# Releasing an expert's weight transfers chunk by chunk in a mixture-of-experts stage

## What is computed

```python
xf = x.reshape(-1, x.shape[-1])
gate_logits = xf @ gate_w.T + gate_b
selected = jnp.argmax(softmax(gate_logits), axis=-1)
out = zeros
for j in range(8):
    yj = xf @ expert_w[j].T + expert_b[j]
    out = out + where((selected == j)[:, None], yj, 0.0)
```

## Time and profile before

| what | value |
|---|---|
| median of 3 runs | 1428.24 us (1428.13 to 1430.22) |
| the profiled execution's own time | 1424.34 us |
| its span, first to last instruction | 1422.7 us |
| mean granted TensorE clock | 0.993 |
| TensorE busy | 1385.2 us, 97% of the span |
| VectorE busy | 1136.3 us, 80% |
| ScalarE busy | 754.9 us, 53% |
| GpSimd busy | 213.2 us, 15% |
| DMA moved | 331.51 MB, 233 GB/s on average |

### The profile page before, as it was taken

The page is one execution under the profiler, slowest core; times in us unless marked ns, Lnnn a source line. Parts: engine busy times, 40 slices in busy tenths (PEclk is TensorE's granted clock), DMA queues, the critical chain, the costliest instruction groups (busy, mean ns, idle before and its releaser), DMA issues.

```text
span 1422.7 us, 20751 instructions
## 1 busy us (share of the span) xinstructions
PE 1385.2 (97%) x6881; PEld 1141.3 (80%) x6881; DVE 1136.3 (80%) x1119; ACT 754.9 (53%) x839; POOL 213.2 (15%) x234
## 2 busy tenths in 40 slices
PE   7899999999999999999999999999999999999996
PEld 7887888888888888888888888888766788788884
DVE  5868887878878788787887878877655799899994
ACT  5656555454554545545455454553204377677772
POOL 0111000000000000000000000000014266564462
PEclk9999999999999999999999999999999999999998
DMA  6864567477774777747676476765858746979951
GB/s 204 328 236 154 203 233 266 169 286 227 255 261 174 285 222 257 258 176 285 220 260 256 177 285 219 261 254 170 293 190 296 277 119 168 336 229 304 344 154 30
DMA packets 102938, 331.51 MB, mean 233 GB/s; under 512 B 15476, under 2 KB 23164, under 8 KB 102876
## 3 DMA queue, kind: packets, MB, share of 16 engines
q1 hardware_dynamic: 79556, 258.56, 49.0%
q0 software_dynamic: 23072, 71.85, 18.0%
q10 hardware_dynamic: 256, 0.40, 0.1%
HBM read 295.63 MB, written 46.14 MB: 240 GB/s over the span
## 4 chain that ended last, share of the span: by engine, by line
PE 91%; DVE 3%; DMA 2%; issue 1%; ACT 1%; ACTq 0%; SPq 0%; DVEq 0%; POOL 0%; POOLq 0%
PE pair L1140 27%; PE pair L1141 26%; PE pair L1142 26%; PE pair L1194 4%; PE pair L1416 1%; PE pair L1342 1%; PE pair L1333 1%; DVE wf L810 1%; DMA wraw<-exp_w 1%; PE pair L1221 1%; PE pair L1278 1%; PE pair L1204 1%; PE pair L1351 1%; PE pair L1383 1%; DVE wlr L1115 1%
## 5 line engine op out<-in xcount | busy, mean ns | idle before, releaser
L810 DVE TENSOR_TENSOR wf<-wf,term 128x1024 f32<-128x1024 f32 x308 | 376.7, 1223 | 65.8 <-ACT term L599 50.7
L599 ACT ACTIVATE term<-codes 128x1024 f32<-128x1024 int32 x308 | 320.6, 1054 | 139.4 <-DVE wf L810 139.4
L1140 PE MATMUL pair<-wh,hh 128*128 128x512 f32 x672 | 263.4, 392 | 3.2 <-DVE ring L873 1.4
L1141 PE MATMUL pair<-wl,hh 128*128 128x512 f32 x672 | 262.0, 390 | 0.0
L1142 PE MATMUL pair<-wh,hl 128*128 128x512 f32 x672 | 262.0, 390 | 0.0
L1140 PE MATMUL pair<-ring,wh 128*128 128x512 f32 x656 | 255.6, 390 | 0.0
L1141 PE MATMUL pair<-ring,wh 128*128 128x512 f32 x656 | 255.3, 389 | 0.0
L1142 PE MATMUL pair<-ring,wl 128*128 128x512 f32 x656 | 255.2, 389 | 0.0
L743 ACT ACTIVATE whr<-wraw 128x1024 fp32r x184 | 188.1, 1056 | 84.3 <-PE pair L1142 48.2
L868 DVE TENSOR_TENSOR acc<-acc,pair 128x1024 f32<-128x1024 f32 x160 | 194.4, 1217 | 47.1 <-PE pair L1142 39.8
L1115 DVE TENSOR_TENSOR wlr<-wraw,whr 128x1024 fp32r<-128x1024 f32 x184 | 213.2, 1220 | 7.8 <-ACT whr L743 7.5
(11 more groups left out here) (180 smaller groups left out, 1510.5 us busy)
## 6 DMA issues: line engine op xcount, KB each, us to landing
ring<-x_parts SPq DMA_DIRECT2D x320, 512.0 KB, 6.5
wraw<-exp_w SPq DMA_DIRECT2D x64, 512.0 KB, 12.1
x_parts<-stage POOLq DMA_DIRECT2D x24, 512.0 KB, 6.5
xg<-exp_b POOLq DMA_DIRECT2D x23, 512.0 KB, 7.9
codes<-codes_up SPq DMA_DIRECT2D x22, 512.0 KB, 6.1
codes<-codes_dn SPq DMA_DIRECT2D x22, 512.0 KB, 5.7
am<-am_dn SPq DMA_DIRECT2D x22, 512.0 KB, 3.9
acc<-x_nat POOLq DMA_DIRECT2D x16, 512.0 KB, 5.4
```

Source lines behind the costliest of these rows:

```text
L599: return nc.scalar.activation(out, codes[:, n % 2], ACT.Relu, scale=scale, bias=-scale * bend)
L810: nc.vector.tensor_tensor(whole(n), whole(n), term[:, e % 2], op).then_inc(term_added, 1)
L1140: mm(ps, ah, bh, start=first, stop=False)
L1141: mm(ps, ah, bl, start=False, stop=False)
```

## The change

SP no longer waits once for all conversions of the last tile of expert e-2. It waits before each chunk kt until the conversion of chunk kt in that tile is counted, and issues that chunk at once. To keep the values positive, `wlr_ready` now starts at 8 (KT) and not at 1, and TensorE's own waits on it are raised by 7, so that they ask for the same conversions as before.

```diff
-            def load_expert(e):
+            def load_expert(e, done=0):
                 for kt in range(KT):
                     if e > 1:
-
+                        sp.wait_ge(wlr_ready, done + kt)
                         sp.wait_ge(wraw_in[e % 2][kt], 16 * (e // 2 + e % 2))
...
-                done = sp.value_load(through[0:1, e - 1:e], min_val=1, max_val=NS * KT + 1)
-                sp.wait_ge(wlr_ready, done)
-                load_expert(e)
+                load_expert(e, sp.value_load(through[0:1, e - 1:e], min_val=1, max_val=NS * KT + 1))
...
-            dve.sem_inc(wlr_ready, 1)
+            dve.sem_inc(wlr_ready, KT)
...
-                    pe.wait_ge(wlr_ready, i * 32 + KT * s + kt + 2)
+                    pe.wait_ge(wlr_ready, i * 32 + KT * (s + 1) + kt + 1)
```

## The result

Faster, by 0.4 to 0.6%.

| comparison | changed kernel, median us (executions) | kernel before | ratio, 95% interval |
|---|---|---|---|
| first | 1419.8 (5) | 1428.13 (5) | 0.9944 [0.9923, 0.9964] |
| `after_again` | 1417.82 (7) | 1427.87 (28) | 0.9939 [0.9917, 0.9962] |
| `after_third` | 1421.89 (12) | 1427.49 (34) | 0.9959 [0.9942, 0.9976] |

The account below looks back on a forecast made before the run. TensorE, 97% busy, was taken as the bound, with a bias-held stall at tile 8. 0.4 us off the profiled 1424.34, plus the median's 3.9 us difference, gave 1427.8 us; range 1423.8 to 1430.4.

Parts of the forecast that it names:

- ScalarE's 8.9 us of waiting: Expert stage: ScalarE's eight waits for weights mostly go, but give nothing, as TensorE waits for none of them.
- The recorded stall and its owner: Ahead of tile 8: TensorE's 2.36 us idle, 4.18 us with clock loss, belongs to tile 6's late bias, not weights.
- The carry to the median: Whole kernel: the median's unexplained 3.9 us above the profiled execution is carried over to the forecast.
- The later loads: Experts 4 to 7: loads start up to 9 us earlier and meet other bias transfers; costed at nothing.
- Expert 3 in expert 2's place: Tile 6's bias: expert 3's early chunks crowd it as expert 2's did, so only 0.4 us is gained.
- a shallow q1: Weight queue with few chunks outstanding beside a busy q0; no row showed whether it would press the bias less.
- `add_rows` waiting over 3 us: Sign that the forecast is right: VectorE still waits over 3 us for tile 6's bias.
- SP's waits: SP's queue: 42 extra waits and additions cost zero, as nothing is queued behind the weights.
- Rival A: Tile 8: the bias lands in time, nearer 6.9 than 11.7 us; 4.18 us saved, 1424.1 us; chance 0.24.
- Rival B: Ahead of tile 8: expert 2's early chunks delay POOL's queue, 2.7 us slower, 1430.9 us; chance 0.13.
- Rival C: SP's issues: register waits pass late or chunks wait anyhow, so loads go as now, 1428.2 us; chance 0.05.

Follow-up runs that it names:

- after_again: The changed kernel, run again unedited for a second profile: 1417.82 us, ratio 0.9939 against the kernel before.
- after_third: The changed kernel, run a third time unedited as the mark for other runs: 1421.89 us, ratio 0.9959 against the kernel before.
- before_again: The kernel before, run again unedited for a second profile: 1428.63 us, ratio 1.0003.
- bias_unwaited: The kernel before with bias transfers sent to a spare tile, so VectorE does not wait for them: 1426.65 us, ratio 1.0017.
- weights_unwaited: The kernel before with the weights of experts 2 to 7 sent to spare chunks that nobody waits for: 1420.54 us, ratio 0.9965.
- after_pool_late: The changed kernel with GpSimd held some 6 us by fills ahead of the gather of tile 8's rows: 1423.24 us, ratio 0.9971.

## Why the prediction was wrong

**The failed step.** "ScalarE's 8.9 us of waiting mostly go and give nothing, as TensorE waits for none of them." True of the stall in the execution shown, and wrong as a price. In it VectorE, which the bias had held until 1224.88, came to chunks 3 to 7 of tile 8 only from 1230.77 on. ScalarE's waits for them ended just ahead of it, and the five low parts ran without a wait:

```profile
1227.68 1.06 ACT L743 ACTIVATE whr<-wraw 128x1024 fp32r x1 [1.40 <-DMA wraw<-exp_w]
1230.24 1.06 ACT L743 ACTIVATE whr<-wraw 128x1024 fp32r x1 [1.50 <-DMA wraw<-exp_w]
1232.92 1.06 ACT L743 ACTIVATE whr<-wraw 128x1024 fp32r x1 [1.62 <-DMA wraw<-exp_w]
...
1230.77 5.76 DVE L1115 TENSOR_TENSOR wlr<-wraw,whr 128x1024 fp32r<-128x1024 f32 x5
```

Where the bias came in time, late weights reached TensorE one tile further on (before_again); with no bias to wait for they do so too (bias_unwaited), and without them most of the gain is there (weights_unwaited). The wait priced at nothing was worth 8.4 of 10.5 us in the second execution. A wait that lies under another looks free; here it was the one that carried the time.

**The recorded stall and its owner.** Read rightly for that execution: with the bias wait gone the step ahead of tile 8 is 11.79. But ScalarE's wait for weights, which I struck out of the chain, was the next in line.

**The carry to the median.** "Nothing in the trace tells why" the median lay 3.9 us above the profiled execution. The second execution lost 5.5 us more in this very stage and less outside it. A profiled execution that is well below the median should have counted as a sign that others hold other stalls.

**The later loads**, costed at nothing because their biases had room. Biases were not what they were short of: ahead of tile 20 the kernel before lost 4.5 us behind expert 7's weights. The run with all loads but expert 2's spread shows that this part alone gains.

**Expert 3 in expert 2's place** was not what the changed kernel's trace shows. The step has nearly all of expert 2 in by 1214, at 1.5 us a chunk; with POOL's queue busy beside it a chunk took 2.9 us on average and the last landed at 1220.95, so tile 6's bias met expert 2 itself. Its consequence held: q1 never ran dry, the two queues moved 385 and 386 packets, the bias took 14.5 us. The step itself can be seen in after_pool_late, where POOL was held: the last five chunks of expert 2 landed 1.3 us apart, all by 1217.66, and the bias issued at 1218.16 shared the engines with expert 3's (426 packets of q0 to 437 of q1 from 1219 to 1228) and took 10.7 us. The rule cited with it, that each DMA engine goes round its queues by packets (the Trainium skill, DMA: Bandwidth & Descriptors, "Queues, rings and completion order"), agrees with these counts too. q1 had 5 or 6 chunks outstanding from 1202 to 1210, as many as in the kernel before from 1216 to 1222, so a shallow q1 isn't shown here either. What didn't follow is "`add_rows` waiting over 3 us": the bias was issued 14.9 us ahead of its use and not 8.1, because POOL's hold fell elsewhere. That was luck as far as the change goes: the hold came before its first early release, and in `before_again`, without the change, the bias left at 1204.45 and was in time too.

**SP's waits** at zero: no run sets them apart, and nothing in the traces speaks against it. **Rival A** foresaw the missing stall at tile 8, but by a bias that lands in nearer 6.9 us than 11.7; it took 14.5. It priced that stall alone, 4.18 us; its 1424.1 lacked the weights as well. **Rival B** named a real sensitivity (the held POOL cost the kernel before 6.3 us in the median, and the changed one 2 to 5 by the ratios), but in no trace here did spread weights cause it. **Rival C** was wrong: the issues do spread.

## What to carry to other kernels

Before a wait on an engine off the critical path is priced at nothing, ask what it would do in an execution in which the wait that now covers it is absent; if the profiled execution lies well off the median, look at a second one first. A prefetch into the only other buffer should be released as each piece of the buffer comes free, above all where the owner of the other buffer is used for one tile only: every stall behind weights here followed such an expert. To find which of two overlapping waits carries the time, take out one at a time and keep the traffic.

## What the runs showed of the hardware

**GpSimd is held behind VectorE's subtractions.** In the first trace of the kernel before 12 of POOL's instructions in the stage take 3.4 to 5.8 us where others like them mostly take 1.0 to 1.2. All 12 begin within a run of low parts (0.9 to 1.2 us after its start) and end 0.89 to 0.95 us after the run's end: the gather of the earlier trace rows from 1204.94 to 1210.77, the run of the earlier trace rows from 1204.07 to 1209.83. The small copy of `zidx` above, 5.30 us from 1175.56, ends within 0.05 us of a run's end. Many more begin inside a run, some of them at the same 0.9 to 1.2 us, and aren't held; what decides it stays open. The Trainium skill (SBUF — State Buffer, "Who interferes with whom") says that a VectorE instruction with two SBUF inputs contends with a GpSimd instruction that reads SBUF; the low parts have two such inputs, and the held copies and the gathers, which take their row numbers from SBUF, agree with that as far as they go. The same section infers that such an instruction leaves the generation of a transfer's descriptors alone; whether that or the reading of the row numbers is held here isn't shown. Which tile is hit changes from one execution of a kernel to the next: the gather at 1204.94, ahead of tile 6's bias, in the first trace before, the one at 1189.47, a gather earlier, in the second. In these two it decides whether that bias is late.

**A low clock ahead of the stage comes and goes.** Windows on TensorE from 58 to 65 us in the kernel before (us, busy, granted clock, DMA share, GB/s):

```profile
58.00:61.00 3.00, 1.51 (x4) 0.50 1.01 414
61.00:65.00 4.00, 4.00 (x11) 0.52 0.84 337
```

The same in the changed kernel:

```profile
58.00:61.00 3.00, 2.38 (x10) 1.00 1.03 422
61.00:65.00 4.00, 4.00 (x19) 1.00 0.60 240
```

In both TensorE had been idle for 3.68 us just before, for `wl` of VectorE. One execution then ran for 6.8 us at about 1.2 GHz, the other at 2.4; `after_again` had 3.4 us of it. Some executions have 3.4 us more near 1113. Over the 14 profiles the span less the stage's loss goes with this: 1414.1 to 1414.5 us with no low clock ahead of the stage, 1415.8 to 1417.3 with 3.4 us of it, 1417.6 to 1419.9 with 6.8, 1418.8 to 1419.7 with 10.2. It is a scatter of nearly 6 us at a place where the change has not acted yet. That it has nothing to do with the change isn't shown, though: the three profiles with no low clock there are all of kernels with the whole change, and the five of such kernels average 1415.3 us, the other nine 1418.0. So of the gains of 5.6 to 10.1 us some 2.8 may lie ahead of the stage (an estimate from these averages), by chance or by the program's other code; no run here tells which.
